# A two-block recurrent kernel on one core: the three condition products in two rounded halves

## The reference, cut to what matters

```python
# block 1
f, i = sigmoid(x @ W_f.T + b_f), sigmoid(x @ W_i.T + b_i)
log_ret = log(f / (f + i + EPS) + EPS)
hidden = cumsum(exp(total - before) * (i / (f + i + EPS)) * (x @ W_h.T + b_h)) + exp(cumsum(log_ret)) * cond
x1 = x + hidden
# block 2: a scan over 128 steps
vz, vr, vh = cond @ C_z + b_z, cond @ C_r + b_r, cond @ C + b
z = sigmoid(x1 @ W_z + h @ U_z + vz)
r = sigmoid(x1 @ W_r + h @ U_r + vr)
h = (1 - z) * h + z * tanh(x1 @ W + (r * h) @ U + vh)
out = x1 + h
```

## Time and profile before

| what | value |
|---|---|
| median of 3 runs | 1526.7 us (1525.97 to 1527.61) |
| the profiled execution's own time | 1527.41 us |
| its span, first to last instruction | 1525.6 us |
| TensorE busy | 1514.2 us, 99% |
| VectorE busy | 1320.9 us, 87% |
| ScalarE busy | 1044.1 us, 68% |
| mean granted TensorE clock | 0.997 |

### The profile page before, as it was taken

One profiled execution on the slowest core, in us unless ns is written; L12 is line 12 of the kernel. 1 busy time (PEld: TensorE's weight loads), 2 busy tenths in 40 slices (PEclk: granted clock), 3 DMA queues, 4 the chain that ended last, 5 costly groups with the idle time before them and its releaser, 6 DMA issues.

```text
span 1525.6 us, 57118 instructions
## 1 busy us (share of the span) xinstructions
PE 1514.2 (99%) x24290; PEld 1174.8 (77%) x24290; DVE 1320.9 (87%) x2921; ACT 1044.1 (68%) x2422; POOL 301.3 (20%) x329
## 2 busy tenths in 40 slices
PE   8999999999999999999999999999999999999998
PEld 6875544444444467777899999999999999999998
DVE  7999889999999889898888888888888888887787
ACT  6989799999999833445566666666665666656333
POOL 0100111111111012322222222222222222222222
PEclk9999999999999999999999999999999999999999
DMA  5056356465638966645333333333333333320000
GB/s 197 28 151 208 83 150 178 115 166 135 186 94 124 121 81 95 81 75 53 46 21 48 48 20 48 21 48 48 20 48 48 21 48 21 48 41 3 32 31 31
DMA packets 544159, 116.80 MB, mean 77 GB/s; under 512 B 520096, under 2 KB 526496, under 8 KB 535200
## 3 DMA queue, kind: packets, MB, share of 16 engines
q1 hardware_dynamic: 536896, 82.73, 31.3%
q0 software_dynamic: 7008, 30.41, 10.6%
HBM read 66.47 MB, written 33.55 MB: 66 GB/s over the span
## 4 chain that ended last, share of the span: by engine, by line
PE 96%; DVE 2%; issue 1%; DMA 0%; ACT 0%; SPq 0%; DVEq 0%
PE ps L1373 33%; PE ps L1475 22%; PE ps L1438 20%; PE ps L1487 12%; PE ps L1459 7%; PE ps L1391 2%; PE ps L1340 1%; DVE ST L1218 0%; DMA raw<-in_x 0%; PE ps L1404 0%; DVE RL L1253 0%; DVE XP L1185 0%; DVE HL L1297 0%; DVE ST L1258 0%; ACT ST L796 0%
## 5 line engine op out<-in xcount | busy, mean ns | idle before, releaser
L1373 PE MATMUL ps<-XH,WH 128*128 128x512 f16 x1872 | 404.7, 379 | 0.0
L1373 PEld LDWEIGHTS ps<-XH,WH 128*128 128x128 f16 x1872 | 183.1, 98 | 220.2 <-issue 0.3
L1475 PE MATMUL ps<-HL,U 128*128 128x64 f16 x7888 | 271.6, 193 | 1.7 <-DVE HL L1297 1.7
L1475 PEld LDWEIGHTS ps<-HL,U 128*128 128x128 f16 x7888 | 255.4, 98 | 9.5 <-issue 3.2
L1586 POOL TENSOR_TENSOR ST<-ST 128x256 f32<-128x256 f32 x127 | 106.3, 837 | 462.7 <-ACT ST L818 462.7
L796 ACT ACTIVATE ST<-ST 128x128 f32<-128x128 f32 x254 | 72.1, 310 | 170.4 <-DVE ST L1218 169.9
L1487 PE MATMUL ps<-HL,U 128*128 128x64 f16 x4064 | 166.5, 195 | 0.0
L1218 DVE SCALAR_TENSOR_TENSOR ST<-ps,dn,AR 128x128 f32<-128x128 f32 (+1 forms) x320 | 109.2, 372 | 44.2 <-PE ps L1487 42.4
L1218 DVE SCALAR_TENSOR_TENSOR ST<-ps,dn,XP 128x128 f32<-128x128 f32 x315 | 107.5, 372 | 42.1 <-PE ps L1487 39.8
L1487 PEld LDWEIGHTS ps<-HL,U 128*128 128x128 f16 x4064 | 141.6, 98 | 0.1
L1475 PEld LDWEIGHTS ps<-RL,U 128*128 128x128 f16 x3824 | 128.1, 98 | 8.0 <-issue 1.2
(11 more groups left out here) (196 smaller groups left out, 2945.2 us busy)
## 6 DMA issues: line engine op xcount, KB each, us to landing
x_scratch<-AR SPq DMA_DIRECT2D x16, 1024.0 KB, 5.3
AR<-in_x POOLq DMA_DIRECT2D x15, 1024.0 KB, 8.0
AR<-HB POOLq DMA_DIRECT2D x11, 1024.0 KB, 7.0
raw<-x_scratch SPq DMA_DIRECT2D x88, 128.0 KB, 4.4
out_y<-raw SPq DMA_DIRECT2D x11, 1024.0 KB, 4.2
raw<-in_x SPq DMA_DIRECT2D x10, 1024.0 KB, 7.4
ST<-in_x SPq DMA_DIRECT2D x5, 1024.0 KB, 7.2
out_y<-AR SPq DMA_DIRECT2D x4, 1024.0 KB, 4.3
```

What stands on the lines that cost most here:

```text
L1373: op = pe.matmul(ps[b][:, :], v[:, g, wp, k, e * P:(e + 1) * P], y[:, xp, k, :], start=n == 0, stop=n == 11)
L1475: pe.matmul(ps[b][:, col:col + B], U[:, g, uh, k, e * P:(e + 1) * P], S[:, k, 0], start=opens, stop=False, skip_group_check=True)
```

## The change

The three condition products are made as the kernel's other products are, out of two halves with three products each, and the halves are of the kind `fp32r`. Each 512 x 512 weight matrix now arrives as plain `f32` in CF (one transfer per condition, in turns 6, 10 and 14) and VectorE makes the halves in CW, in four pieces per condition: `high 0` and `low 0` at the end of the second turn, `high 1` at the end of the third, `low 1` at the end of the fourth (12 pieces over the three conditions; a piece spans two of the four contraction tiles, 128 x 1024). The halves of `cond` itself (CS) are made once, at the end of turn 6. The products move from turns 8, 9, 10 to turns 10, 14, 18, and each has 48 matmuls of 128 x 64 instead of 16. The core of the diff:

```diff
-        CW = over("CW", w_at + 24576, 6144).rearrange("p (g k n) -> p g k n", g=3, k=KT)
+        CF = over("CF", w_at + 24576, 2048).rearrange("p (k n) -> p k n", k=KT)
+        CW = over("CW", w_at + 24576 + 8192, 4096, F32R).rearrange("p (h k n) -> p h k n", h=2, k=KT)
+        CS = over("CS", ar_at + 4 * 11776, 512, F32R).rearrange("p (h k b) -> p h k b", h=2, k=KT)
...
-        C_PAIR = {2 * WIDE + 2: 1, 2 * WIDE + 3: 2, 2 * WIDE + 4: 0}
+        C_PAIR = {2 * WIDE + 4 * n + 4: g for n, g in enumerate(C_ORDER)}
+        def c_split_turn(q):
+            n, s = divmod(q - 2 * WIDE, 4)
+            return (n, ([], ["high 0", "low 0"], ["high 1"], ["low 1"])[s]) if 0 <= n < 3 else (None, [])
...
-                if q == 2 * WIDE:
-                    sp.wait_ge(s_mm[2], 4 * WIDE)
-                    for g in C_ORDER:
-                        sp.dma_start(CW[:, g], by_k(staged[C_STAGE[g]])).then_inc(d_stage[C_STAGE[g]], 16)
+                n, parts = c_split_turn(q)
+                if n is not None and not parts:
+                    if n:
+                        sp.wait_ge(s_clo, 2 * n + 1)
+                    else:
+                        sp.wait_ge(s_mm[2], 4 * WIDE)
+                    sp.dma_start(CF, by_k(staged[C_STAGE[C_ORDER[n]]])).then_inc(d_cw, 16)
...
+            def conditions():
+                dve.wait_ge(d_cond, 16)
+                dve.tensor_copy(CS[:, 0], CT).then_inc(s_chi, 1)
+                dve.wait_ge(s_chi, 1)
+                dve.tensor_tensor(CS[:, 1], CT, CS.bitcast(F32)[:, 0], ALU.subtract).then_inc(s_clo, 1)
+            def c_split(n, part):
+                half = int(part[-1])
+                k = slice(2 * half, 2 * half + 2)
+                if part == "high 0":
+                    dve.wait_ge(d_cw, 16 * (n + 1))
+                    if n:
+                        dve.wait_ge(s_cmm, n)
+                if part[:-2] == "high":
+                    dve.tensor_copy(CW[:, 0, k], CF[:, k]).then_inc(s_chi, 1)
+                else:
+                    dve.wait_ge(s_chi, 2 * n + half + 2)
+                    dve.tensor_tensor(CW[:, 1, k], CF[:, k], CW.bitcast(F32)[:, 0, k], ALU.subtract).then_inc(s_clo, 1)
...
                 candidate(2 * q + 1)
                 if q and (q - 1) // 2 in DIRECT:
                     finish(q - 1)
+                n, parts = c_split_turn(q)
+                if n == 0 and not parts:
+                    conditions()
+                for part in parts:
+                    c_split(n, part)
...
             def condition(g):
-                b, n = bank("v", g), C_STAGE[g]
-                s = CW[:, g]
-                pe.wait_ge(d_cond, 16)
-                pe.wait_ge(d_stage[n], 16)
+                b, n = bank("v", g), C_ORDER.index(g)
+                pe.wait_ge(s_chi, 2 * n + 3)
+                pe.wait_ge(s_clo, 2 * n + 3)
                 wait_bank(pe, "v", g)
                 for e in range(KT):
-                    for k in range(KT):
-                        op = pe.matmul(ps[b][:, e * B:(e + 1) * B], s[:, k, e * P:(e + 1) * P], CT[:, k, :],
-                                       start=k == 0, stop=k == KT - 1)
+                    for i in range(12):
+                        (wp, cp), k = PRODUCTS[i // KT], i % KT
+                        op = pe.matmul(ps[b][:, e * B:(e + 1) * B], CW[:, wp, k, e * P:(e + 1) * P], CS[:, cp, k],
+                                       start=i == 0, stop=i == 11)
```

More of the change, by code:

```diff
@@ L67, in build @@
         raw01 = sb("raw01", 2 * 2048)
+        ar_at = -(-nc.sbuf_base // 32) * 32
         AR = sb("AR", 16768)
@@ L193, in build @@
         d_b1, d_cond, d_b2 = sem("d_b1"), sem("d_cond"), sem("d_b2")
-        d_stage = {n: sem(f"d_stage_{n}") for n in range(3, 12)}
+        d_stage = {n: sem(f"d_stage_{n}") for n in range(3, 12) if n not in (CR, CZ, CH)}
+        d_cw, s_chi, s_clo = sem("d_cw"), sem("c_hi"), sem("c_lo")
         d_x1d = [sem("d_x1d_0"), sem("d_x1d_1")]
```

## The result

The changed kernel takes 1592.9 us (median of 4 runs, 1592.29 to 1593.19), the kernel before 1526.5 beside it (4 runs): a ratio of 1.0432, with a 95% interval of 1.042 to 1.0444, so 66.4 us slower. The forecast was 1580.4 with a range of 1565 to 1598.

The account below looks back on a forecast made before the run. TensorE's list of work was taken to bound the kernel. Products 5.3, waits 40.9 and clock 7.5 sum to 53.7 us on the profiled 1527.4, so 1581.1, with the median 0.7 lower at 1580.4 us; range 1565 to 1598.

Parts of the forecast that it names:

- The bound and the direction: Stage one is as long as TensorE's work; added work and waits arrive in full; slower by over 3 us has 97%.
- the high end: Top of the forecast range, 1598 us: waits of 43.5, products 5.3 and clock loss 23, together 72 us.
- dear casts: VectorE's high halves: casts of 1.17 us instead of the 0.74 taken, growing the waits to 43.5 us.
- the case that I had held likeliest: Whole kernel: 5.3 us products, 40.9 us waits and 7.5 us clock loss, giving 1580.4 us; chance 60%.
- The wait: TensorE before conditions in turns 10, 14, 18: waits for VectorE's `low 1`, 14.9, 13.0 and 13.0 us, sum 40.9.
- the lag is a debt paid once: Rival on the conditions' waits: after the first, VectorE keeps up and later ones vanish; 22.7 us added, 1549.4; 5%.
- The products' own price: TensorE's conditions: 48 `fp32r` products at 110 ns, 5.28 us each, 1.76 more than before, +5.3 us in all.
- The cheaper price of a half record: Rival on the condition products: 55 ns each, 2.64 us a condition, 1572.5 us in all; 17%.
- the reading of the passes: Condition products: four passes per true FP32 product, one per `fp32r`, so 55 ns a pass and 2.6 us a condition.
- the clock's term: After each new TensorE wait: 5 us of work at half pace, 2.5 us lost each, +7.5 us in all.
- the clock stays low: Rival: half clock over the whole condition and some of the turn behind, 7.8 us each instead of 2.5; 1596 us; 13%.
- Two of my signs: Changed profile: 48 records in 5.3 us at full clock; granted clock at 0.5 for some 5 us after each wait.

## Why the prediction was right, and where it was not

**The bound and the direction: right.** TensorE's list of work set stage one, and all that was added to it arrived at the end: 66.2 us in the rows, 66.4 in the times.

**The range.** 1592.9 lies inside 1565 to 1598, but 12.5 us above the likeliest number. It is inside because the high end had taken in the low clock at 23 us, together with dear casts that did not come; the case that I had held likeliest, at 60%, is not the one that came.

**The wait: right, mechanism and size.** 14.9, 13.0 and 13.0 us were forecast, 14.5, 12.6 and 12.6 came. The cast took 0.68 us where 0.74 was taken, which is part of the small excess, and `low 1` starts right behind the last candidate. The two kernels in which TensorE asks later or VectorE delivers earlier have no wait at all. The rival that the lag is a debt paid once is refuted: VectorE had 23 us of idle time in turn 10, and was late by 12.6 us again in turn 13.

**The products' own price: right.** 5.28 us a condition at full clock, as taken from the weight loads. The cheaper price of a half record, 2.64 us, is refuted, and with it the reading of the passes in the Trainium skill ("FP8 and Floating Point Precision", section "TensorE Precision Notes") that I had made for this case: an `f32` record of 64 columns and an `fp32r` product cost the same 110 ns here. What sets the 110 ns was not isolated; with `fp16` halves, whose weight loads are the short ones, the same 48 products take 1.40 us.

**The step that failed is the clock's term.** It stood at 2.5 us for each wait, 7.5 in all, read off the one idle stretch of the trace before. Measured: the conditions took 10.42 us instead of 5.28, and the turns behind lost 2.2, 1.2 and 2.4 us, 21.2 us in all. That is the rival "the clock stays low", to which I had given 13% and 7.8 us a condition; measured, 7.1. Two of my signs did not come: 48 records in 5.3 us at full clock, and a low clock for only some 5 us after each wait (14.8 us after the first). The row that I used was the wrong model because the work that followed that idle stretch was 512 columns wide, whereas here 48 products of 64 columns come first, and these do not bring the clock back, in 10.4 us or in 20.7. My argument against the rival, that stage two runs on 64-column `fp16` products at full clock, spoke of products at 29 ns and not at 110. The term was also charged to the waits alone: the two kernels without any wait lose 6.7 and 6.8 us to the clock in their chains all the same, so the unbroken stretch of these products has a price of its own, which the sum put at nothing. The 13.7 us missing in that term, less 1.2 that the waits were overestimated by, are the 12.5 us between 1580.4 and 1592.9.

**What stays open.** What share of the 21.2 us the stretch itself would have cost behind the idle waits was not separated. Why plain `f32` products at the same pace keep the clock and `fp32r` ones lose it was not tried further, nor was how an `fp32r` stretch wider than 64 columns stands, apart from the 512 columns of chunks 0 to 2, which run at the full clock.

## What to carry to other kernels

Before an operand is handed from one engine to another, look up in the timeline how far behind the maker runs at that place in its program, not how busy it is: an engine with a tenth of idle time can deliver nearly a whole turn late (14.5 of 15.54 us here), and the bounding engine then pays the lag in full, each time. Price a wait of the matrix engine together with what it does right after the wait, since the clock comes back by the work that follows and that work may be of a kind that does not bring it back, or that loses it when it runs unbroken. And an emulation of exact products by three rounded ones is cheap or dear by the kind of its halves: the same 48 products took 5.28 us in `fp32r` and 1.40 us in `fp16`.

## What the runs showed of the hardware that was not expected

- In an unbroken stretch of 48 `fp32r` products of 64 columns (5.3 us, no idle time in the rows), or within 0.2 us of its end, the granted clock fell to 0.50, in all six such stretches of the two kernels without a wait, and the 512-column products behind it paid 1.4 to 2.8 us each time; split into four stretches of 12 it kept 1.00 (1531.5 against 1540.0 us).
- 96 such products after an idle wait ran all of their 20.66 us at 1.2 GHz.
- 64 records of plain `f32` products in 7.09 us, at the same 110 ns, kept 2.4 GHz.
- The Trainium skill, page "TensorE: Matmul & The Clock Gate", section "HAM oscillation", speaks of idle gaps as what sends a kernel back to the low clock. The changed kernel agrees: the clock falls to 0.50 at 2.0, 4.8 and 3.8 us into its three waits. In the kernel with the earlier low half it falls with no gap in the rows, at 177, so here gaps were not the only way.
